# A four-layer network of 128x128 pixels on one core: bias of the norm in column tiles, attention and last layer reordered

## The reference

```python
# layer 0: attention along rows, 4 heads of 32, over a second norm of each pixel
x = _layernorm(pair, gamma, beta)
q = (x @ Wq) * SCALING; k = x @ Wk; v = x @ Wv      # reshaped by head
bias = x @ Wb                                       # one number per pixel and head
gate = sigmoid(x @ Wg + bg)
attn = softmax(einsum('bijhd,bikhd->bijkh', q, k) + bias[:, None], axis=-2)
out = (gate * einsum('bijkh,bikhd->bijhd', attn, v)) @ Wo + bo
# layer 1: a window attention and a 3x3 depthwise convolution
# layer 2: per row a correlation, its top 9, and 8 Runge-Kutta steps; relu
# layer 3: products of X and of its transpose, of row, column and diagonal means
ret = L(X, 10) + L(X.transpose(0, 2, 1, 3), 11)
ret = ret + (L(rows, 6) + L(cols, 8) + L(diag, 12))[:, :, None, :]
ret = ret + (L(rows, 7) + L(cols, 9) + L(diag, 13))[:, None, :, :]
ret = ret + 2.0 * L(sum_diag, 14)[:, None, None, :]
ret = ret + diag_term[:, :, None, :] * eye          # of kinds 1 to 5
out = relu(ret @ Wm + bm)
```

## Time and profile before

| | us |
|---|---|
| median of 3 runs | 1188.38 (1185.97 to 1188.86) |
| the profiled execution | 1187.14 |
| its span | 1185.3 |
| PE busy | 1092.6 (92%) |
| DVE, ACT, POOL busy | 743.1, 520.7, 341.0 |
| chain that ended last | the output loop of layer 3, from 1141.56 |

### The profile page before, as it was taken

The page is one execution under the profiler, slowest core; times in us unless marked ns, Lnnn a source line. Parts: engine busy times, 40 slices in busy tenths (PEclk is TensorE's granted clock), DMA queues, the critical chain, the costliest instruction groups (busy, mean ns, idle before and its releaser), DMA issues. The chain is left out here.

```text
span 1185.3 us, 25594 instructions
## 1 busy us (share of the span) xinstructions
PE 1092.6 (92%) x9547; PEld 783.1 (66%) x9547; DVE 743.1 (63%) x3576; ACT 520.7 (44%) x1113; POOL 341.0 (29%) x477
## 2 busy tenths in 40 slices
PE   4898999999999699949999999999999999999688
PEld 3457777777777334437767777677677677677486
DVE  3673777778778522245676676766766766766235
ACT  2364767676676300024444445444444444443200
POOL 0151656665665210000221221221212212212211
PEclk8796999999999889958999999999999999999869
DMA  8000000000000000000000000000000000000012
GB/s 165 1 1 1 2 3 2 2 3 2 2 3 2 1 1 1 1 10 1 1 1 1 2 1 2 1 1 1 1 1 2 1 1 1 1 1 1 1 40 108
DMA packets 10463, 11.09 MB, mean 9 GB/s; under 512 B 3812, under 2 KB 8164, under 8 KB 10340
## 3 DMA queue, kind: packets, MB, share of 16 engines
q1 hardware_dynamic: 8964, 8.87, 2.8%
q10 hardware_dynamic: 1376, 0.59, 0.3%
HBM read 5.14 MB, written 4.23 MB: 8 GB/s over the span
## 5 line engine op out<-in xcount | busy, mean ns | idle before, releaser
L1498 PE MATMUL quad<-theta,nat 128*128 128x512 f32 x512 | 240.7, 593 | 0.0
L669 POOL TENSOR_TENSOR nat<-nat,arena 128x512 f32<-128x512 f32 x128 | 132.6, 1047 | 127.2 <-DVE arena L733 127.2
L1297 POOL TENSOR_TENSOR nat<-nat,const 128x512 f32<-128x512 f32 x32 | 40.6, 1270 | 439.8 <-DVE nat L1436 439.8
L1506 PEld LDWEIGHTS quad<-flat 128*128 128x128 f32 x768 | 104.6, 190 | 46.4 <-ACT flat L1328 25.0
L1498 PEld LDWEIGHTS quad<-theta,nat 128*128 128x128 f32 x512 | 87.5, 191 | 61.7 <-issue 61.7
L1506 PE MATMUL quad<-flat 128*128 128x128 f32 x768 | 123.8, 284 | 2.8 <-ACT flat L1328 1.7
L733 DVE CUSTOM_DVE_ANT_0 nat<-quad,arena 128x128 f32<-128x128 f32 x512 | 113.2, 282 | 7.0 <-PE quad L823 7.0
L1328 ACT ACTIVATE flat<-quad 128x256 f32<-128x256 f32 x192 | 73.3, 382 | 70.6 <-PE quad L1506 56.7
L692 ACT ACTIVATE nat<-bank 128x512 f32<-128x512 f32 x128 | 69.5, 595 | 56.9 <-PE bank L831 56.9
L1405 DVE SCALAR_TENSOR_TENSOR flat<-nat,c,duo 128x128 f32<-128x128 f32 x64 | 22.1, 345 | 101.9 <-PE duo L1515 101.9
L697 ACT ACTIVATE nat<-nat 128x512 f32<-128x512 f32 x128 | 77.3, 634 | 5.6 <-POOL nat L669 5.5
(11 more groups left out here) (390 smaller groups left out, 2271.8 us busy)
## 6 DMA issues: line engine op xcount, KB each, us to landing
out<-nat SPq DMA_DIRECT2D x16, 256.0 KB, 2.0
const<-in_constants ACTq DMA_DIRECT2D x1, 400.5 KB, 3.2
arena<-in_L_conv_Ws SPq DMA_DIRECT2D x1, 240.0 KB
flat<-arena SPq DMA_DIRECT2D x3, 32.0 KB, 4.5
nat<-in_x SPq DMA_DIRECT2D x4, 0.2 KB, 12.0
arena<-in_L_conv_Wq ACTq DMA_DIRECT2D x1, 32.0 KB, 6.7
arena<-in_L_conv_Wk ACTq DMA_DIRECT2D x1, 32.0 KB, 6.4
arena<-in_L_conv_Wv ACTq DMA_DIRECT2D x1, 32.0 KB, 6.1
```

The lines of the kernel that those rows point to most:

```text
L669: pool.tensor_tensor(scored, scored, of_head(least[b], h).broadcast_to([128, ROWS, L]), ALU.subtract).then_inc(lowered, 1)
L1297: pool.tensor_tensor(quarters(rem), quarters(rem), ident.unsqueeze(1).broadcast_to([128, ROWS, 128]), ALU.add).then_inc(diag_added, 1)
L1498: return pe.matmul(m.quad[:, n, :], vT[:, col(n)], m.theta[:, part, :], start=(part == 0), stop=False, skip_group_check=True)
L1506: last = pe.matmul(m.quad[:, row, place * C:(place + 2) * C], a8[g % 2][:, col(row)], zs[half][k % 2][:, n, :], start=False, stop=(k == 2) ...
```

## The change

Opening: `keep_weights` is parted; the products are kept after the second doubling, the biases after the third, so VectorE's first four measurements (L281) come sooner. GpSimd clears `w0b`.

Norm of layer 0: the two products for the powers move from ahead of the loop to behind its third step, and the setup of layer 1 moves back by three steps. GpSimd multiplies banks 0 to 7, VectorE 8 to 15. The 128 products of the bias are replaced, behind the loop, by four chunks: four products of 32 columns (one per quarter of the partitions) with four banks of `z` moving, a copy to SBUF, four transposes, and an addition of the head's bias. The attention then begins with `bias_turned` in place.

Attention: the reciprocal in VectorE and the widening copy in GpSimd are put ahead of the step's first head; TensorE transposes the widened reciprocals ahead of the fourth turn of the exponentials.

Last layer: the column sums move into the block of the last group norm, on GpSimd (with their scaling), and so do the raw rows and the diagonal, on VectorE. The two blocks become one. TensorE makes the spread weights and the column term first, then the own products of two steps, then the other totals. The transfers are issued part by part.

```diff
-                dve.wait_ge(S("a_w0_made"), 1)
+            def keep_products():
+                dve.wait_ge(S("a_early_made"), 3)
                 dve.tensor_scalar(m.w0[:, 0:128], m.bank[4][:, 0:128], float(1.0 / np.sqrt(HD)), None, ALU.mult)
                 dve.tensor_copy(m.w0[:, 128:512], m.bank[4][:, 128:512])
-                dve.wait_ge(S("a_w0b_made"), 1)
-                step(dve.memset(m.w0b[:, :], 0.0))
+
+            def keep_biases():
+                dve.wait_ge(S("a_early_made"), 4)
+                dve.wait_ge(S("a_cleared"), 1)
                 for half in range(2):
...
-                if i == 0:
-                    keep_weights()
                 measure(([0] + MEASURED_BY)[i], MEASURED_BY[i])
+                if i == 1:
+                    keep_products()
+                if i == 2:
+                    keep_biases()
...
+def group_norm(nc, m, layer, loads=(), loaded=None, pool_aside=None, dve_aside=None):
...
 
+        @block.gpsimd
+        def _(pool):
+            if pool_aside is not None:
+                pool_aside(pool)
+
...
+            if dve_aside is not None:
+                dve_aside(dve)
...
+    m.bias_turned, bias_raw = (m.flat[:, L * L // 2 + n * CH:L * L // 2 + (n + 1) * CH] for n in range(2))
...
-    POOL_SCALES = BATCH_ENDS[1]
+    POOL_SCALES = 8
...
-            for at in range(2):
-                act.wait_ge(last_made, at + 1)
-                act.activation(m.pw[:, 17 + 8 * at:25 + 8 * at, :], m.quad[:, 2 + at, :].rearrange("p (j e) -> p j e", e=C),
-                               ACT.Copy).then_inc(last_kept, 1)
...
+                if p == 0:
+                    for at in range(2):
+                        act.wait_ge(early_made, at + 1)
+                        act.activation(m.pw[:, 17 + 8 * at:25 + 8 * at, :], m.quad[:, 2 + at, :].rearrange("p (j e) -> p j e", e=C),
+                                       ACT.Copy).then_inc(last_kept, 1)
...
-            for at in range(2):
-                pe.matmul(m.quad[:, 2 + at, :], m.power_turn, m.pw[0:C, 1 + 8 * at:9 + 8 * at, :], start=True, stop=True).then_inc(last_made, 1)
...
+                if q == 2:
+                    for at in range(2):
+                        pe.matmul(m.quad[:, 2 + at, :], m.power_turn, m.pw[0:C, 1 + 8 * at:9 + 8 * at, :],
+                                  start=True, stop=True).then_inc(early_made, 1)
...
-                for bank in range(*BIAS_AFTER.get(q, (0, 0))):
-                    if bank < POOL_SCALES:
-                        pe.wait_ge(z_ready, bank + 1)
-                    else:
-                        pe.wait_ge(late_z_ready, bank + 1 - POOL_SCALES)
-                    for pair in range(4 * bank, 4 * bank + 4):
-                        last = pe.matmul(m.quad[:, 2, pair * 8:(pair + 1) * 8], m.z[:, pair * L:(pair + 1) * L], m.w0b[:, :],
-                                         start=True, stop=True)
-                    if bank == BANKS - 1:
-                        last.then_inc(bias_made, 1)
+                    pe.matmul(m.quad[0:C, 3, 128:129], m.turned1[0:C, 192:256], m.dw_b, start=True, stop=True).then_inc(early_made, 1)
+            for chunk in range(CHUNKS):
+                if 4 * chunk < POOL_SCALES:
+                    pe.wait_ge(z_ready, 4 * chunk + 4)
+                else:
+                    pe.wait_ge(late_z_ready, 4 * chunk + 4 - POOL_SCALES)
+                if chunk > 0:
+                    pe.wait_ge(bias_kept, 2 * chunk)
+                for t in range(4):
+                    last = pe.matmul(m.quad[32 * t:32 * (t + 1), 2, :], m.w0b[:, :], m.z[:, cols(4 * chunk + t)],
+                                     start=True, stop=True, skip_group_check=True)
+                last.then_inc(bias_made, 1)
+                pe.wait_ge(bias_kept, 2 * chunk + 1)
+                for pair in range(4):
+                    last = pe.transpose(m.quad[:, 2, pair * L:(pair + 1) * L], bias_raw[:, pair * L:(pair + 1) * L], ident)
+                last.then_inc(bias_made, 1)
...
+            def keep_bias(chunk):
+                dve.wait_ge(bias_made, 2 * chunk + 1)
+                dve.tensor_copy(bias_raw, m.quad[:, 2, :]).then_inc(bias_kept, 1)
+                dve.wait_ge(bias_made, 2 * chunk + 2)
+                of_pairs = m.quad[:, 2, :].rearrange("p (pair t x) -> p t pair x", pair=4, t=4)[:, :, :, 0:2 * HEADS]
+                dve.tensor_tensor(m.bias_turned[:, chunk * L:(chunk + 1) * L].rearrange("p (t pair x) -> p t pair x", t=4, pair=4), of_pairs,
+                                  m.head_bias[:, :].unsqueeze(1).unsqueeze(1).broadcast_to([128, 4, 4, 2 * HEADS]),
+                                  ALU.add).then_inc(bias_kept, 1)
+
...
-            scale(POOL_SCALES, BANKS)
+            scale(POOL_SCALES, 12)
+            keep_bias(0)
+            keep_bias(1)
+            scale(12, BANKS)
+            keep_bias(2)
+            keep_bias(3)
...
+                if g >= 2:
+                    pool.wait_ge(rtotal_ready, g - 1)
+                    if g > 2:
+                        pool.wait_ge(r_made, g - 2)
+                    pool.tensor_copy(rwide.rearrange("p (x d) -> p x d", d=HD),
+                                     rtotal.unsqueeze(2).broadcast_to([128, ROWS * HEADS, HD])).then_inc(rwide_ready, 1)
...
-                    if h == 0 and g >= 2:
-                        pool.wait_ge(rtotal_ready, g - 1)
-                        if g > 2:
-                            pool.wait_ge(r_made, g - 2)
-                        pool.tensor_copy(rwide.rearrange("p (x d) -> p x d", d=HD),
-                                         rtotal.unsqueeze(2).broadcast_to([128, ROWS * HEADS, HD])).then_inc(rwide_ready, 1)
...
-                if own:
-                    dve.wait_ge(scores_made, g + 1)
-                    if g >= 2:
-                        dve.wait_ge(turned, 4 * (g - 1))
-                    shift_head(g, b, 0)
                 if older:
                     dve.wait_ge(sums_turned, g - 1)
                     if g >= 3:
                         dve.wait_ge(rwide_ready, g - 2)
                     dve.reciprocal(rtotal.rearrange("p (r h) -> p r h", r=ROWS),
                                    total_bank[:, 0:128].rearrange("p (r x) -> p r x", r=ROWS)[:, :, 0:HEADS]).then_inc(rtotal_ready, 1)
+                if own:
+                    dve.wait_ge(scores_made, g + 1)
+                    if g >= 2:
+                        dve.wait_ge(turned, 4 * (g - 1))
+                    shift_head(g, b, 0)
...
-                    for r in range(2, ROWS):
-                        pe.wait_ge(kept, 4 * (g - 1) + r - 1)
-                        turn(g - 1, r)
+                    pe.wait_ge(kept, 4 * (g - 1) + 1)
+                    turn(g - 1, 2)
...
+                if past:
+                    pe.wait_ge(kept, 4 * (g - 1) + 2)
+                    turn(g - 1, 3)
...
+    def sums_of_cols(pool):
+        step = m.chain(pool, "pool")
+        step(pool.memset(both[C:128, C:2 * C], 0.0))
+        step(pool.tensor_copy(both[0:C, C:2 * C], ident64))
+        step(pool.tensor_tensor(col_half, m.colsum[:, 0:L], m.colsum[:, L:2 * L], ALU.add))
+        step(pool.tensor_copy(cols_raw, col_half[C:128, :]))
+        step(pool.tensor_tensor(cols_raw, cols_raw, col_half[0:C, :], ALU.add))
+        step(pool.tensor_scalar(cols_raw, cols_raw, 1.0 / L, None, ALU.mult))
+
+    def raw_rows(dve):
+        for e in range(2):
+            dve.tensor_scalar(rows_raw[:, e:L:2], m.rowsum[e * C:(e + 1) * C, :], 1.0 / L, None, ALU.mult)
+        dve.tensor_copy(diag_raw, m.img[0:C, 0:L * L:L + 1])
+
+    group_norm(nc, m, 3, pool_aside=sums_of_cols, dve_aside=raw_rows)
...
+            pool.wait_ge(S("flattened"), 16 * 3)
...
+            dve.tensor_scalar(spread_scale, ident64, m.scale2[0:C, :], None, ALU.mult).then_inc(prepared, 1)
+            dve.tensor_scalar(rows_x, rows_raw, m.scale2[0:C, :], m.shift2[0:C, :], ALU.mult, ALU.add)
+            dve.tensor_scalar(cols_x, cols_raw, m.scale2[0:C, :], m.shift2[0:C, :], ALU.mult, ALU.add)
+            dve.tensor_scalar(diag_x, diag_raw, m.scale2[0:C, :], m.shift2[0:C, :], ALU.mult, ALU.add).then_inc(prepared, 1)
+            dve.wait_ge(terms_made, 1)
+            dve.tensor_copy(both[:, 0:C], B[1][:, 0:C]).then_inc(prepared, 1)
+            dve.wait_ge(terms_made, 2)
+            step(dve.tensor_copy(of_col, B[2][:, 0:C]))
...
+                dve.tensor_copy(part, m.rounded[:, :]).then_inc(split_ready, 1)
+                dve.wait_ge(split_ready, n + 1)
...
+            step(dve.tensor_reduce(mean_diag, diag_x, AX.X, ALU.add))
+            step(dve.tensor_reduce(mean_all, rows_x, AX.X, ALU.add))
+            step(dve.tensor_scalar(mean_diag2, mean_diag, 2.0 / L, None, ALU.mult))
+            step(dve.tensor_scalar(mean_diag, mean_diag, 1.0 / L, None, ALU.mult))
+            dve.tensor_scalar(mean_all, mean_all, 1.0 / L, None, ALU.mult).then_inc(prepared, 1)
+            dve.wait_ge(terms_made, 3)
```

(43 more changed lines are left out.)

177 lines of the change are left out of this document (53 added, 124 removed).

## The result

The changed kernel takes 1157.45 us (median of four runs, 1155.92 to 1160.30) against 1188.11 of the kernel before in the same comparison: ratio 0.975, 95% interval 0.972 to 0.977. That is 30.7 us less where 17.3 were predicted; 1157.45 lies under the low end of the range, 1163. The direction and all four places were right, the size was not. Its profiled run took 1155.92 us with a span of 1154.1.

The account below looks back on a forecast made before the run. TensorE was taken to bound the first attention, with time also lost in the opening, norm tail and last stage; -2.9 -3.0 -8.1 -3.3 = -17.3 us from 1187.14 gave 1169.8, stated as 1170.5, range 1163 to 1180.

Parts of the forecast that it names:

- The opening: Opening: first transposed power copied 3.3 us sooner, as four banks are measured before products are kept; -2.9 us, bounds -3.3 and -1.5.
- The norm: Norm of layer 0: earlier loop start and four chunks replacing the products behind it give -3.0 us, bounds -6.7 and +7.
- the half-clock choice: Norm's tail: TensorE idles ahead of the chunks, so mostly half clock taken, 4.4 us a chunk instead of 2.8.
- The attention: Attention: TensorE's wait for GpSimd's widened reciprocals goes, steps 8.97 to 8.70 us; -8.1 us, bounds -9.3 and +13.
- VectorE's delay: Attention: VectorE's head 0 comes at 204.6 instead of 204.20; at worst 0.42 us in each of 31 steps, +13.
- The bound of -9.3: Attention: the most it could give, all 31 waits of TensorE for the widened copy, 9.3 us by the rows.
- The last stage: Last stage: own products sooner by 7.5 us, less 3.7 for GpSimd's load and 0.5 for the clock; -3.3, bounds -7.5 and +1.5.
- Rival (a): Last stage's load costs nothing (-7.5), or norm's tail runs at full clock (-6.7): about 1167 us, down to 1163; chance 0.20.
- (b): Attention: the wait only changes its name, to VectorE's head shifts or ScalarE's fourth turn; total -9.2, 1179 us; chance 0.15.
- (c): Norm: the 32-column products run one after another, +7 instead of -3, 1181 us; chance 0.04.
- (e): Last stage: GpSimd's code load is longer than 5.0 us, 1 us more for the stage, 1171.5 us; chance 0.14.
- (d): Attention: reciprocal ahead of head 0 makes VectorE the bound, +13 against -9.2, so +3.8, 1192 us; chance 0.05.

Follow-up runs that it names:

- n1: The kernel before with only the change's opening and norm of layer 0, attention and last stage as before: ratio 0.994, 6.8 us less.
- a2: The kernel before with only VectorE's and GpSimd's attention order changed (reciprocal and widened copy first), TensorE's order untouched: ratio 0.987, 15.9 us less.
- x1: The changed kernel with the four transposes of the reciprocals moved between the second and third turn: ratio 0.975 to the kernel before, as the changed kernel.
- a3: The kernel before with only TensorE's attention order changed, four transposes ahead of the fourth turn, GpSimd's copy still late: ratio 1.009, 11.2 us more.
- x5: The changed kernel with x1's order and the sums transposed ahead of the last eight scores of each step: ratio 0.974 to the kernel before.
- x2: The changed kernel with the ones-row products of last-stage steps 0 and 1 between the two long totals: ratio 0.977 to the kernel before.
- x7: The changed kernel with x2's order and the second step's own products in two halves between the totals' records: ratio 0.976 to the kernel before.
- x6: The changed kernel with bank 11 scaled behind chunks 0 and 1, and 64 unread transposes in TensorE's norm and attention-start waits: ratio 0.972 to the kernel before.
- x11: The changed kernel with x1's turn order, x6's scalings and transposes, and unread transposes ahead of the last stage: ratio 0.969 to the kernel before, 1151.4 us.
- x12: x11 with x2's order of the last stage too: ratio 0.971 to the kernel before.

## Why the prediction was wrong in size

- **The opening**: -2.9 predicted, -2.7 and -1.8 in two profiles, -3.4 between the means of all. Right.
- **The norm**: -3.0 predicted, -4.1 and -2.3, with -1.5 at the attention's start in the first profile alone. The mechanism and the half-clock choice held; the size less so: four profiles with the old norm take 56.5 to 57.3 us, eight of the nine with the new one 55.0 to 55.7, so the usual gain is nearer 1.5. n1's 6.8 for opening and norm is 0.9 above the sum of the two terms.
- **The attention, the step that failed**: "each of 30 even steps shrinks by the 0.27". The wait did go, nothing came late in its place, VectorE's delay cost nothing. But the price was read from the matmul's row, 0.27. The weight load's row said 0.51, and a2, with TensorE's own order untouched, gave 0.50; with TensorE's new order it is 0.54. The stage gave 16.5 instead of 8.1. The bound of -9.3, "all waits", was too narrow for the same reason.
- **The last stage, the second error**: 3.7 us were charged for a load of GpSimd's code by a row that gave only an upper bound, and it cost 0.1 at most. The Trainium skill's figure for the first call of fresh code (GPSIMD Engine Reference, "Instruction dispatch"), about 6 us, is not borne out here either: the tensor-scalar starts at once. Rival (a) was right on this. The clock was charged 0.5 and took 1.66 in the third step's own products, which came 6.8 us sooner than before and not 7.5, since the totals took 0.7 more than charged. Together -7.5 + 0.7 + 1.66 = -5.1 for -3.3.
- **The rivals**: (b), a wait that only changes its name, did not happen in the change; it is what x1 met. (c), products one after another, and (e), a longer load, fell by the rows above. (d), slower, did not happen with both halves in place; a3 shows that the slower side was real by another road.
- **The sum** by what was measured: 2.7 + 4.1 + 16.5 + 5.1 and 1.5 for the start is 29.9, and 1.3 in code that was not changed. Between this 31.2 and the forecast 17.3 lie 13.9 us: 8.4 are the attention's price, 1.8 the last stage, 1.1 the norm, 1.5 its start and 1.3 the unchanged code, less 0.2 of the opening. That the result missed the range is the attention's price: without its 8.4 it would stand near 1166.
- **Two sums that do not close** in the prediction, without weight in the result: (c)'s +7 would be about +11 by its own terms (three chunks at 6.8 instead of 2.1 on top of 2.7 less), and the last stage with its totals at half clock -2.4, not -2.8.

## What to carry over

Price a wait of TensorE by the spacing of starts against a place with no wait, not by the idle time of the matmul's row. The weight load's row is the quick reading, and a little high: it said 0.51 where 0.50 came back (a2) and 0.46 where 0.37 did (x5), the matmul's row 0.27 and 0.21. A wait that goes can still be paid elsewhere: x1 changed its name, and x5 lost it in a change of the kind of product. When one queue is reordered, ask what the copy it waits for does first: TensorE's half of this change alone made the kernel 0.9% slower. Profile a kernel twice before a few us at a place with a changing clock are counted as a gain.

## Of the hardware

- A wait of TensorE behind transposes of 128 columns cost more than its matmul row shows: 0.27 us shown and 0.50 given back in a2, 0.21 shown and 0.37 given back in x5.
- The clock also falls with TensorE busy: 5.97 and 6.00 of the 6 us up to the fall in x2 and x7, where 64 by 64 records and own products follow each other. Why is open. In the norm of the changed kernel it falls by pauses, and 64 short transposes in them and in the attention's start keep it up (x6, x11, x12).
- The clock's phase differs from run to run of one program: 72.2 us for norm and start in one profile of the changed kernel, 75.6 in the other.
- One transpose of 128 rows among products of 32 rows costs 0.30 us more than behind them (x5's 1.57 us against x1's 1.27).
- GpSimd's second load of its code shows with 4 ns in the trace of the changed kernel, and the operations on both sides of it lie 0.09 us apart.
